# Fourier steps among conv2 in four groups instead of six, with changes of the prologue and of the work in front of conv2

## Chip, cores and metric

One core of a Trainium2 chip (trn2) runs the whole program. The metric is the device time of one execution in microseconds (us). TensorE (PE) does matrix products, VectorE (DVE) and ScalarE (ACT) elementwise work and copies out of PSUM, GpSimd (POOL) a part of the products of the prologue, SyncE (SP) issues most DMAs.

## Reference

x has 8 images of 32 channels of 64 x 64, float32. A first stage makes nine weights per pixel and blends each pixel's 3 x 3 neighbours with them; then come four layers (DEPTH = 4).

```python
# L0: h = leaky_relu(conv3x3(x, w1) + b1, 0.2)
#     w_lp = softmax(conv1x1(h, w2) + b2, axis=1)         # 9 weights a pixel
#     x = x + sum_k shift_k(x) * (delta_centre - w_lp[k])
for j in range(4):                                        # L1
    Kj, Lj = project(K[j]), project(L[j])                 # less their 3x3 mean
    z = relu(batchnorm(conv3x3(x, Kj), gamma[j], beta[j]))
    x = batchnorm(x + 0.1 * conv3x3T(z, Kj), gamma[j], beta[j])
    # diag_imp_conv_fft:
    t = 1.0 / (0.1 * abs(fft2(pad(Lj))) ** 2 + 1.0)
    x = real(ifft2(fft2(x) * t))
```

## The kernel before

The 8 images are taken as 4 pairs (bp), each pair in 4 quarters (q), so a stage has 16 chunks c = 4 bp + q (NCH = 16). The partitions hold 4 row groups (R) of 32 channels. X0 and Z0 hold x and z, X2 and Z2 copies that are shifted by two row groups (a DMA makes them), so that a 3 x 3 convolution of a chunk is 12 products of 128 rows by 32 columns, four of them side by side in the array (`conv`, L887; 24 MATMUL records a chunk).

Every product goes to one of 8 PSUM banks. The steps are numbered (`NUMBER`) in the order in which PE issues them; step n uses bank n % 8 and waits (`claim`) until step n - 8 is drained. The order is written by hand: `prologue_order` for the first stage and `layer_steps(j)` for a layer. Every engine walks the same list and does its own part of each step, so the list sets the order on PE, DVE and ACT alike.

**Prologue.** `hidden` p is the 3x3 convolution of two chunks (L910), `logits` the 1x1 one (L926), `less_max`, `exps` and `probabilities` make the softmax, which `cut` splits in three bf16 parts; `probsT` turns them (L939), `spread` copies each weight over the 32 channels by a product of 32 rows (L949), DVE and POOL multiply (L723, L421), and `sum` adds the 12 products of a chunk (L961). conv1 of layer 0 runs five chunks behind (BEHIND). SP and ACT issue the loads of x; b1 is loaded behind the first eight loads of SP (L353), and PE waits for `hconv_consts` 32 (w1 and b1) before its first product. ACT's order at the start is `keep_hidden(0)`, `keep_hidden(1)`, `exps(0)`, three `cut`s, `keep_probs(0)` and `(1)` (L486 to L493).

**A layer.** conv1 (16 chunks; DVE takes the statistics), with `prepare_taps` on DVE behind its seventh chunk. Then four `table` products (L987) of the filter's transform, each 12 rows by 128 columns by 512, with the product that spreads the means (`norm` 1, L995) in their middle. `scale_and_bias` on DVE (with a root on ACT) gives scale and bias of the batch norm; ReLU of z is then done in place, on ACT by `relu_pair` (L543), and for the shifted rows of the first chunk on DVE by `relu_first` (L800, L801). ACT squares the tables (L523), and DVE's `make_table` adds them and takes the reciprocal of 1,024 columns (L806 to L808), ahead of its first `add_conv2`. conv2 follows (L887 again; DVE adds the result to x, L815, and takes statistics, L818). Among its chunks stand the Fourier steps of the pairs that are done: `turn` (transpose, L1012, kept by ACT at L555), `fwdW` (transform along W, L1023), `fwdH` (along H, L1039, with `slot0`, L1032, in front and `slot0c`, L1047, behind it; DVE multiplies by the table), `invH` (L1057), `invW` (L1068). fwdW and invH come out of a bank in four copies a quarter (`keep_moved`: L568 on ACT, L824 on DVE); `by_dve` says who does it: DVE for fwdW of pairs 0 and 1 and the even quarters of the others, and for the odd quarters of invH of pairs 1 to 3. There is one buffer each for turned data (`turned`), the spectrum along W (`freqw`) and the whole spectrum (`spec`), and two for the way back (`backw`). Behind conv2 comes the second norm, whose scale `invW` (on ACT, L583) needs.

```python
    after = {
        5: fourier(j, 0, "turn"),
        7: fourier(j, 0, "fwdW"),
        9: fourier(j, 0, "fwdH") + fourier(j, 1, "turn"),
        11: fourier(j, 0, "invH") + fourier(j, 1, "fwdW"),
        13: fourier(j, 1, "fwdH") + fourier(j, 2, "turn"),
        15: fourier(j, 1, "invH") + fourier(j, 2, "fwdW"),
    }
```

## Time and profile before

| | us |
|---|---|
| median of 3 runs (lowest, highest) | 787.32 (786.62, 787.52) |
| the profiled execution, its own time | 783.87 |
| its span in the profile | 782.0 |
| PE busy | 741.6 (95%) |
| DVE busy | 479.6 (61%) |
| ACT busy | 387.5 (50%) |
| POOL busy | 95.6 (12%) |
| mean granted TensorE clock | 0.972 of full |
| prologue, up to the last conv1 of layer 0 | about 0 to 179.4 |
| a layer from its tables to the next layer's | about 158.7 |

The busy share says how long an engine had an instruction in flight, not that it ran at its peak. The granted clock is given as a share of 2.4 GHz: 1.00 is 2.4 GHz and 0.50 is 1.2 GHz, and a stretch between is a mixture of the two. Idle time is put down to what ended it.

### The profile page before, as it was taken

How to read it: one execution, taken by the hardware profiler on the slowest of the kernel's cores; microseconds unless marked ns; L12 is line 12 of the kernel's file. 1: busy time of each engine (PE TensorE's matmuls, PEld its weight loads, DVE VectorE, ACT ScalarE, POOL GpSimd, SP SyncE). 2: the span in 40 equal slices, each digit the busy share in tenths (PEclk: the TensorE clock that was granted, in tenths of full speed). 3: DMA queues.
4: the chain of work that ended last, by engine and by line, in shares of the span. 5: the costliest groups of instructions: out<-in, count | busy, mean ns of one | idle time of the engine just before them, and what ended most of it. 6: DMA issues, size and time to landing. Idle time of an engine off the chain costs nothing.

```text
span 782.0 us, 14876 instructions
## 1 busy us (share of the span) xinstructions
PE 741.6 (95%) x6016; PEld 374.5 (48%) x6016; DVE 479.6 (61%) x911; ACT 387.5 (50%) x703; POOL 95.6 (12%) x92
## 2 busy tenths in 40 slices
PE   4779999999999999999999999999999999999995
PEld 1223333222454875224558753235677542355785
DVE  2587887764957852448668533397676333877661
ACT  1465666636622655257135543491446433823564
POOL 0376666830000000000000000000000000000000
PEclk9798999999999999989999999999999998999998
DMA  9991111248000132840000427500004274000034
GB/s 182 188 164 29 29 30 28 56 92 191 2 1 1 31 80 61 187 118 2 1 1 1 110 56 166 145 1 1 1 2 111 55 166 110 1 1 1 2 88 129
DMA packets 44645, 51.16 MB, mean 65 GB/s; under 512 B 36385, under 2 KB 36514, under 8 KB 42530
## 3 DMA queue, kind: packets, MB, share of 16 engines
q1 hardware_dynamic: 40098, 48.92, 29.1%
q10 hardware_dynamic: 4480, 1.30, 1.1%
q8 instruction: 49, 0.80, 0.4%
q14 instruction: 18, 0.15, 0.1%
HBM read 11.92 MB, written 4.19 MB: 21 GB/s over the span
## 4 chain that ended last, share of the span: by engine, by line
PE 81%; DVE 10%; ACT 3%; issue 2%; DMA 1%; SPq 1%; POOL 0%; DVEq 0%; ACTq 0%; POOLq 0%
PE psum L887 39%; PE psum L1068 7%; PE psum L1039 7%; PE psum L961 6%; PE psum L1057 6%; PE psum L1023 6%; PE psum L910 3%; PE psum L1012 2%; PE psum L949 2%; DVE work L824 2%; DVE tabT L808 2%; DVE spare L824 2%; ACT Z L543 1%; PE psum L926 1%; DVE X L815 1%
## 5 line engine op out<-in xcount | busy, mean ns | idle before, releaser
L887 PE MATMUL psum<-Z,wts 128*32 128x512 f32 x1536 | 177.4, 615 | 5.1 <-DVE Z L801 5.1
L887 PE MATMUL psum<-X,wts 128*32 128x512 f32 x1536 | 170.1, 593 | 0.2 <-DMA X<-X 0.2
L824 DVE COPY work<-psum 64x256 f32<-64x256 f32 x224 | 94.5, 422 | 22.9 <-PE psum L1023 15.9
L734 DVE BATCH_NORM_STATS2 stats<-Z 128x6 f32<-128x512 f32 x60 | 41.5, 692 | 106.8 <-ACT Z L483 106.7
L887 PEld LDWEIGHTS psum<-Z,wts 128*32 128x32 f32 x1536 | 49.5, 112 | 118.3 <-issue 107.6
L887 PEld LDWEIGHTS psum<-X,wts 128*32 128x32 f32 x1536 | 47.4, 109 | 105.5 <-issue 103.1
L483 ACT ACTIVATE Z<-psum 128x512 f32<-128x512 f32 x64 | 38.3, 598 | 118.1 <-PE psum L887 107.0
L543 ACT ACTIVATE Z<-Z,small 64x128 f32<-64x128 f32 (+3 forms) x92 | 85.0, 973 | 5.2 <-DVE small L792 4.7
L568 ACT ACTIVATE work<-psum 64x256 f32<-64x256 f32 x160 | 61.4, 384 | 34.7 <-PE psum L1057 22.5
L815 DVE SCALAR_TENSOR_TENSOR X<-psum,X 128x512 f32<-128x512 f32 x64 | 43.7, 683 | 47.4 <-PE psum L887 47.0
L1057 PEld LDWEIGHTS psum<-cstS,work 128*128 128x128 f32 x512 | 58.4, 192 | 9.8 <-issue 9.8
L1057 PE MATMUL psum<-cstS,work 128*128 128x128 f32 x512 | 61.0, 277 | 0.5 <-ACT work L561 0.5
L1023 PE MATMUL psum<-cstS,work 128*128 128x128 f32 x512 | 60.2, 276 | 0.0
L1023 PEld LDWEIGHTS psum<-cstS,work 128*128 128x128 f32 x512 | 58.4, 192 | 3.4 <-issue 3.4
L561 ACT ACTIVATE work<-psum 128x64 f32<-128x64 f32 x16 | 4.6, 286 | 106.6 <-PE psum L1047 106.6
L1039 PE MATMUL psum<-work,cstS 128*128 128x496 f32 x128 | 56.3, 583 | 0.0
L842 DVE TENSOR_TENSOR work<-psum,tabT 128x496 f32<-128x496 f32 x64 | 41.2, 669 | 8.4 <-PE psum L1039 8.1
L818 DVE BATCH_NORM_STATS2 stats<-X 128x6 f32<-128x512 f32 x64 | 44.4, 694 | 2.2
L723 DVE TENSOR_TENSOR spare<-Z,psum 128x512 f32<-128x512 f32 x60 | 38.5, 679 | 11.9 <-PE psum L949 9.8
L723 DVE TENSOR_TENSOR work<-Z,psum 128x512 f32<-128x512 f32 x52 | 33.6, 680 | 16.0 <-PE psum L949 15.4
L583 ACT ACTIVATE X<-psum,small 128x512 f32<-128x512 f32 x48 | 36.1, 777 | 8.9 <-DVE small L792 3.6
L568 ACT ACTIVATE spare<-psum 64x256 f32<-64x256 f32 x64 | 24.9, 388 | 27.4 <-PE psum L1057 26.8
(104 smaller groups left out, 874.1 us busy)
## 6 DMA issues: line engine op xcount, KB each, us to landing
X<-X SPq DMA_DIRECT2D x64, 260.0 KB, 3.8
Z<-Z SPq DMA_DIRECT2D x32, 520.0 KB, 7.1
Z<-x SPq DMA_DIRECT2D x36, 128.0 KB, 5.0
out<-Z SPq DMA_DIRECT2D x24, 128.0 KB, 2.3
parS<-par SPq DMA_DIRECT2D x4, 673.0 KB, 8.2
Z<-x SPq DMA_DIRECT2D x12, 120.0 KB, 5.1
Z<-x ACTq DMA_DIRECT2D x14, 64.0 KB, 4.2
Z<-x SPq DMA_DIRECT2D x14, 64.0 KB, 4.8
```

The lines of the kernel that those rows point to most:

```text
L543: last = nc.scalar.activation(z, z, ACT.Relu, bias=small[p0:p1, 13:14], scale=small[p0:p1, 12:13])
L568: last = nc.scalar.activation(dst, src, ACT.Identity)
L723: nc.vector.tensor_tensor(by_line(product(c, dj, r)), around(c, dj, r), by_line(bank(n)), op=ALU.mult)\
L815: nc.vector.scalar_tensor_tensor(xc, in0=by_row(bank(n)), scalar=STEP, in1=xc, op0=ALU.mult, op1=ALU.add).then_inc(drained[n % BANKS], 1)
L818: return nc.vector.bn_stats(stats[:, 6 * c:6 * c + 6], xc)
L824: last = nc.vector.tensor_copy(dst, src)
L887: last = nc.tensor.matmul(out_b[C * r:C * r + C, :], weights[:, o:o + C], rows(src, reg, bp, g, CH, dj - 1), start=(dj == 0), stop=(dj == ...
L961: last = nc.tensor.matmul(bank(n)[C * r:C * r + C, :], cm(C_STACK, C), product(c, dj, r), start=(dj == 0), stop=(dj == 2), tile_position=( ...
L1023: last = nc.tensor.matmul(bank(n)[:, 128 * i:128 * i + 128], turned[:, p:p + 128], cm(C_FW), start=True, stop=True)
L1039: nc.tensor.matmul(bank(n)[:, 0:16 * (SL - 1)], cm(C_FH), freqw[:, N * q:N * q + N].rearrange("p (a s) -> p a s", s=SL)[:, :, 1:SL], start ...
L1057: last = nc.tensor.matmul(bank(n)[:, 128 * cp:128 * cp + 128], spec[:, p:p + 128], cm(C_IH), start=True, stop=True)
L1068: last = nc.tensor.matmul(bank(n)[:, 128 * g:128 * g + 128], backw[bp % 2][:, p:p + 128], cm(C_IW), start=True, stop=True)
```

## The change

1. Prologue. A product with w1 alone is issued 16 times (WARM) before PE waits for anything but w1; w1 gets a semaphore of its own. ACT runs one Prelu on a single column as soon as b1 is there. ACT does `keep_hidden(1)` behind the cuts of half 0 instead of ahead of `exps(0)`. The third `hidden` step moves from the end of chunk 0 to the middle of chunk 1 (HIDDEN_BEHIND), on PE and on ACT.
2. The taps and the table products use all 128 partitions; those beyond 12 hold zeros.
3. ReLU of the first pair is in three pieces, of 4, 4 and 8 row groups: ACT takes Z0, DVE all whole rows of Z2. conv2's chunks 0, 1 and 2 wait for a piece each.
4. `make_table` is split. `add_squares` stands behind chunk 0 of conv2, and the reciprocal is in four pieces of 256 columns behind chunks 1, 3, 5 and 6. `slot0` waits for all four. ACT waits for `squares_read` where it waited for `table_done`.
5. Fourier steps stand behind chunks 5, 9, 13 and 15 of conv2.

```diff
+INVERT_BEHIND = (1, 3, 5, 6)
+WARM = 16
+HIDDEN_BEHIND = (1, *range(2, 2 * PAIRS - 4, 2))
@@ def prologue_chunk(c):
+    if c == HIDDEN_BEHIND[0]:
+        order.append(("hidden", 2))
     order += spreads(c, 2)
-    if c % 2 == 0 and c // 2 + 2 < PAIRS:
-        order.append(("hidden", c // 2 + 2))
+    if c in HIDDEN_BEHIND[1:]:
+        order.append(("hidden", HIDDEN_BEHIND.index(c) + 2))
@@ def layer_steps(j):
         5: fourier(j, 0, "turn"),
-        7: fourier(j, 0, "fwdW"),
-        9: fourier(j, 0, "fwdH") + fourier(j, 1, "turn"),
-        11: fourier(j, 0, "invH") + fourier(j, 1, "fwdW"),
-        13: fourier(j, 1, "fwdH") + fourier(j, 2, "turn"),
-        15: fourier(j, 1, "invH") + fourier(j, 2, "fwdW"),
+        9: fourier(j, 0, "fwdW") + fourier(j, 1, "turn"),
+        13: fourier(j, 0, "fwdH") + fourier(j, 1, "fwdW") + fourier(j, 2, "turn"),
+        15: fourier(j, 0, "invH") + fourier(j, 1, "fwdH") + fourier(j, 2, "fwdW") + fourier(j, 1, "invH"),
@@ sync
-            sp.dma_start(w1S[:, :], w1).then_inc(hconv_consts, 16)
+            sp.dma_start(w1S[:, :], w1).then_inc(w1_in, 16)
@@ scalar
-            act.wait_ge(hconv_consts, 32)
+            act.wait_ge(hconv_consts, 16)
+            nc.scalar.activation(small[:, 24:25], b1S[:, 0:1], ACT.Prelu, alpha=LEAK)
             keep_hidden(0)
-            keep_hidden(1)
             exps(0)
             for i in range(3):
                 cut(0, i)
+            keep_hidden(1)
@@ def norm_relu(bp, g, n):
                 if g == 0:
                     parts.append((Z2, REG2, 0, 1, 2 * C, 128))
...
+                if bp:
+                    parts.append((Z2, REG2, g + 1, min(n, G - 1 - g), 0, 128))
+                if g + n == G:
+                    parts.append((Z2, REG2, G, 1, 0, 2 * C))
@@ def relu_pair(j, bp):
                 norm_relu(bp, 0, CH)
-                norm_relu(bp, CH, G - CH)
+                if bp == 0:
+                    norm_relu(bp, CH, CH)
+                    norm_relu(bp, 2 * CH, G - 2 * CH)
+                else:
+                    norm_relu(bp, CH, G - CH)
@@ vector: def relu_first(j)
-                z = rows(Z2, REG2, 0, 1, CH)
-                link(nc.vector.tensor_scalar(z, z, S(12), S(13), ALU.mult, ALU.add))
-                nc.vector.tensor_scalar(z, z, 0.0, None, ALU.max).then_inc(relu_by_dve, 1)
+                for g, n in ((1, CH), (1 + CH, CH), (1 + 2 * CH, G - 1 - 2 * CH)):
+                    z = rows(Z2, REG2, 0, g, n)
+                    link(nc.vector.tensor_scalar(z, z, S(12), S(13), ALU.mult, ALU.add))
+                    nc.vector.tensor_scalar(z, z, 0.0, None, ALU.max).then_inc(relu_by_dve, 1)
...
+            def invert(i):
+                t = tabT[:, 256 * i:256 * i + 256]
+                nc.vector.reciprocal(t, t).then_inc(table_done, 1)
@@ vector: steps of a layer
-                        make_table(j)
                     elif what == "conv2":
                         ins = add_conv2(*at)
+                        if at[1] == 0:
+                            add_squares(j)
+                        elif at[1] in INVERT_BEHIND:
+                            invert(INVERT_BEHIND.index(at[1]))
@@ tensor
+            pe.wait_ge(w1_in, 16)
+            for i in range(WARM):
+                nc.tensor.matmul(bank(NUMBER["logits", 1])[0:3 * C, 0:3 * C], w1S[:, :], w1S[:, :], start=True, stop=True)
             pe.wait_ge(zeroed, 1)
-            pe.wait_ge(hconv_consts, 32)
+            pe.wait_ge(hconv_consts, 16)
@@ def table(j, i):
-                nc.tensor.matmul(bank(n), cm(e, k=12), taps[:, N * (i % 2):N * (i % 2) + N], start=True,
+                nc.tensor.matmul(bank(n), cm(e), taps[:, N * (i % 2):N * (i % 2) + N], start=True,
@@ def conv2(j, c):
-                if c == 0:
-                    pe.wait_ge(relu_by_dve, j + 1)
-                if c % Q < 2:
-                    pe.wait_ge(relu_done, 2 * BP * j + 2 * (c // Q) + 1 + c % Q)
+                bp, q = divmod(c, Q)
+                if bp == 0 and q < 3:
+                    pe.wait_ge(relu_by_dve, 3 * j + q + 1)
+                    pe.wait_ge(relu_done, (2 * BP + 1) * j + q + 1)
+                elif q < 2:
+                    pe.wait_ge(relu_done, (2 * BP + 1) * j + 2 * bp + q + 2)
```

How it moves instructions: PE among conv2 of a layer, from the tables to the second norm. `X,wts` is conv1 and `Z,wts` conv2 (x12 is one chunk), `cstS,X` turn, `cstS,work` of L1023 fwdW and of L1057 invH, 128x496 fwdH, 128x64 slot0 or slot0c, `small` a norm. Before:

```order
L887 MATMUL psum<-Z,wts 32x512 x72
L1012 MATMUL psum<-cstS,X 128x128 x16
L887 MATMUL psum<-Z,wts 32x512 x24
L1023 MATMUL psum<-cstS,work 128x128 x16
L887 MATMUL psum<-Z,wts 32x512 x24
L1032 MATMUL psum<-work,cstS 128x64
L1039 MATMUL psum<-work,cstS 128x496 x4
L1047 MATMUL psum<-work,cstS 128x64
L1012 MATMUL psum<-cstS,X 128x128 x16
L887 MATMUL psum<-Z,wts 32x512 x24
L1057 MATMUL psum<-cstS,work 128x128 x16
L1023 MATMUL psum<-cstS,work 128x128 x16
```

And after, where fwdW is L1057, turn L1046, fwdH L1073 and invH L1091, from the second group to the second norm's step:

```order
L915 MATMUL psum<-Z,wts 32x512 x48
L1057 MATMUL psum<-cstS,work 128x128 x16
L1046 MATMUL psum<-cstS,X 128x128 x16
L915 MATMUL psum<-Z,wts 32x512 x48
L1066 MATMUL psum<-work,cstS 128x64
L1073 MATMUL psum<-work,cstS 128x496 x4
L1081 MATMUL psum<-work,cstS 128x64
L1057 MATMUL psum<-cstS,work 128x128 x16
L1046 MATMUL psum<-cstS,X 128x128 x16
L915 MATMUL psum<-Z,wts 32x512 x24
L1091 MATMUL psum<-cstS,work 128x128 x16
```

Between two groups PE now does four conv2 chunks (x48) where it did two (x24), and the last group behind chunk 15 starts with invH of pair 0. ACT's start of the program, before:

```order
L437 ACT_TABLE_LOAD
L437 ACTIVATE work<-psum,b1S 128x512 x2
L443 ACTIVATE work<-work 128x288
L450 ACTIVATE work<-work 128x32x9 x3
L457 ACTIVATE work<-psum 128x512 x2
```

And after (with the tiles' numbers kept apart: work0 takes `keep_hidden`, work1 `exps`, work3 the cuts and `keep_probs`):

```order
L498 ACT_TABLE_LOAD
L498 ACTIVATE small<-b1S 128x1
L447 ACTIVATE work0<-psum,b1S 128x512
L453 ACTIVATE work1<-work1 128x288
L460 ACTIVATE work3<-work2 128x32x9 x3
L447 ACTIVATE work0<-psum,b1S 128x512
L467 ACTIVATE work3<-psum 128x512 x2
```

The table load has gone ahead of the first `keep_hidden`, and the second `keep_hidden` behind the three cuts.

## Rows read from the trace of the kernel before

**Rows 1.** The page: PE's busy time, and the chain that ended last, by engine.
```profile
PE 741.6 (95%) x6016; PEld 374.5 (48%) x6016; DVE 479.6 (61%) x911; ACT 387.5 (50%) x703; POOL 95.6 (12%) x92
...
PE 81%; DVE 10%; ACT 3%; issue 2%; DMA 1%; SPq 1%; POOL 0%; DVEq 0%; ACTq 0%; POOLq 0%
```

**Rows 2.** Busy time by stretch: start:end, length, PE, PEld, DVE, ACT, POOL; then PEclk.
```profile
184.90:188.30 3.40, 3.17 (x16) 0.90 (x20) 0.00 (x0) 3.37 (x4) 0.00 (x0) 0.50 1.00 213
...
338.50:341.90 3.40, 3.40 (x10) 1.33 (x8) 2.42 (x12) 0.89 (x2) 0.00 (x0) 1.00 0.37 78
341.90:348.70 6.80, 5.56 (x25) 1.35 (x28) 1.37 (x4) 6.29 (x9) 0.00 (x0) 0.50 0.82 219
```

**Rows 3.** Timeline of PE, fronts of conv2, layers 0 to 3: start us, length us.
```profile
185.13 17.21 PE L887 MATMUL psum<-Z,wts 128*32 128x512 f32 x144 [1.50 <-DVE Z L801]
...
203.98 0.63 PE L1012 MATMUL psum<-cstS,X 128*128 128x128 f32 x4 [0.18 <-DVE X L815]
...
343.78 18.09 PE L887 MATMUL psum<-Z,wts 128*32 128x512 f32 x144 [1.24 <-DVE Z L801]
...
502.95 17.02 PE L887 MATMUL psum<-Z,wts 128*32 128x512 f32 x144 [1.51 <-DVE Z L801]
...
661.60 17.90 PE L887 MATMUL psum<-Z,wts 128*32 128x512 f32 x144 [0.86 <-DVE Z L801]
```

**Rows 4.** The chain that ended last, layer 0: start us, length us, what.
```profile
209.90 3.77 PE psum L1023 x32
...
218.96 0.40 PE psum L1032 x2
...
222.87 1.75 PE psum L1012 x16
...
233.68 3.57 PE psum L1023 x32
...
248.22 5.33 PE psum L887 x48
...
263.49 3.34 PE psum L1039 x8
...
312.25 25.90 PE psum L887 x240
```

**Rows 5.** Groups by line: busy us, mean ns | idle before, releaser.
```profile
L824 DVE COPY work<-psum 64x256 f32<-64x256 f32 x224 | 94.5, 422 | 22.9 <-PE psum L1023 15.9 <-PE psum L1057 3.3
...
L568 ACT ACTIVATE work<-psum 64x256 f32<-64x256 f32 x160 | 61.4, 384 | 34.7 <-PE psum L1057 22.5 <-PE psum L1023 10.3
...
L815 DVE SCALAR_TENSOR_TENSOR X<-psum,X 128x512 f32<-128x512 f32 x64 | 43.7, 683 | 47.4 <-PE psum L887 47.0
...
L555 ACT ACTIVATE work<-psum 128x512 f32<-128x512 f32 x64 | 33.3, 602 | 9.7 <-PE psum L1012 9.6
...
L808 DVE RECIPROCAL tabT<-tabT 128x1024 f32<-128x1024 f32 x4 | 26.2, 6553 | 0.1
...
L800 DVE TENSOR_SCALAR Z<-Z,small 128x512 f32<-128x512 f32 x4 | 2.2, 548 | 0.1
```

**Rows 6.** Timeline of ACT, front of conv2 in layer 0.
```profile
183.71 4.85 ACT L543 ACTIVATE Z<-Z,small 128x512 f32<-128x512 f32 x5 [1.18 <-DVE small L792]
```

**Rows 7.** The chain that ended last, start of the program.
```profile
9.92 4.93 PE psum L910 x24
14.93 1.28 ACT L437
...
16.96 1.40 PE psum L926 x8
...
23.18 0.34 ACT work L443
...
28.87 0.61 PE psum L949
```

**Rows 8.** The page: loads of x in half groups, KB each, us to landing.
```profile
Z<-x SPq DMA_DIRECT2D x14, 64.0 KB, 4.8
```

More of the change, by code:

```diff
@@ L168, in build @@
         turned, freqw, spec, rest, backw0 = work
-        taps = rest[0:12, 0:C * SL]
+        taps = rest[:, 0:C * SL]
         slot0 = rest[:, C * SL:C * SL + 2 * C]
@@ L185, in build @@
         ksum = sb("ksum", 2 * C)
-        lsum = sb("lsum", 6 * C, parts=12)
+        lsum = sb("lsum", 6 * C)
         extra = sb("extra", N)
@@ L213, in build @@
         drained = [sem(f"bank_drained{i}") for i in range(BANKS)]
+        w1_in = sem("w1_in")
         hconv_consts = sem("hconv_consts")
@@ L241, in build @@
         relu_done = sem("relu_done")
+        squares_read = sem("squares_read")
         table_done = sem("table_done")
@@ L506, in _ @@
                     keep_conv1(0, c - BEHIND)
+                if c == HIDDEN_BEHIND[0]:
+                    keep_hidden(2)
                 copy_weights(c, 2)
@@ L509, in _ @@
                     cut(c // 2 + 1, 0)
-                if c % 2 == 0 and c // 2 + 2 < PAIRS:
-                    keep_hidden(c // 2 + 2)
+                if c in HIDDEN_BEHIND[1:]:
+                    keep_hidden(HIDDEN_BEHIND.index(c) + 2)
                 if c % 2 and c + 1 < NCH:
@@ L648, in prepare_taps @@
                 al, be = lsum[:, 4 * C:5 * C], lsum[:, 5 * C:6 * C]
-                link(nc.vector.tensor_reduce(ml, parS[0:12, P_L9:P_ALL].rearrange("p (c t) -> p c t", t=TAPS),
+                link(nc.vector.tensor_reduce(ml, parS[:, P_L9:P_ALL].rearrange("p (c t) -> p c t", t=TAPS),
                                              op=ALU.add, axis=AX))
-                link(nc.vector.scalar_tensor_tensor(row, in0=ml.unsqueeze(2).broadcast_to([12, C, 3]), scalar=-1.0 / TAPS,
-                                                    in1=parS[0:12, P_L:P_L9].rearrange("p (c t) -> p c t", t=3),
+                link(nc.vector.scalar_tensor_tensor(row, in0=ml.unsqueeze(2).broadcast_to([128, C, 3]), scalar=-1.0 / TAPS,
+                                                    in1=parS[:, P_L:P_L9].rearrange("p (c t) -> p c t", t=3),
                                                     op0=ALU.mult, op1=ALU.add))
-                nc.vector.tensor_scalar(al, row[:, :, 1], cstS[0:12, C_ONE:C_ONE + 1], None, ALU.mult)
-                link(nc.vector.scalar_tensor_tensor(be, in0=row[:, :, 0], scalar=cstS[0:12, C_SGN:C_SGN + 1],
+                nc.vector.tensor_scalar(al, row[:, :, 1], cstS[:, C_ONE:C_ONE + 1], None, ALU.mult)
+                link(nc.vector.scalar_tensor_tensor(be, in0=row[:, :, 0], scalar=cstS[:, C_SGN:C_SGN + 1],
                                                     in1=row[:, :, 2], op0=ALU.mult, op1=ALU.add))
                 t3 = taps[:, :].rearrange("p (c s) -> p c s", s=SL)
-                link(nc.vector.tensor_tensor(t3, be.unsqueeze(2).broadcast_to([12, C, SL]),
-                                             cstS[0:12, C_CS:C_CS + SL].unsqueeze(1).broadcast_to([12, C, SL]),
+                link(nc.vector.tensor_tensor(t3, be.unsqueeze(2).broadcast_to([128, C, SL]),
+                                             cstS[:, C_CS:C_CS + SL].unsqueeze(1).broadcast_to([128, C, SL]),
                                              op=ALU.mult))
-                nc.vector.tensor_tensor(t3, t3, al.unsqueeze(2).broadcast_to([12, C, SL]), op=ALU.add)\
+                nc.vector.tensor_tensor(t3, t3, al.unsqueeze(2).broadcast_to([128, C, SL]), op=ALU.add)\
                     .then_inc(prep_done, 1)
@@ L798, in relu_first, with add_squares @@
                 dve.wait_ge(z2_in[0], 32 * (j + 1))
-                z = rows(Z2, REG2, 0, 1, CH)
-                link(nc.vector.tensor_scalar(z, z, S(12), S(13), ALU.mult, ALU.add))
-                nc.vector.tensor_scalar(z, z, 0.0, None, ALU.max).then_inc(relu_by_dve, 1)
-            def make_table(j):
+                for g, n in ((1, CH), (1 + CH, CH), (1 + 2 * CH, G - 1 - 2 * CH)):
+                    z = rows(Z2, REG2, 0, g, n)
+                    link(nc.vector.tensor_scalar(z, z, S(12), S(13), ALU.mult, ALU.add))
+                    nc.vector.tensor_scalar(z, z, 0.0, None, ALU.max).then_inc(relu_by_dve, 1)
+            def add_squares(j):
                 for i in range(4):
                     bk.result(NUMBER["table", j, i])
-                link(nc.vector.tensor_tensor(tabT[:, :], turned[:, 0:1024], turned[:, 1024:2048], op=ALU.add))
+                nc.vector.tensor_tensor(tabT[:, :], turned[:, 0:1024], turned[:, 1024:2048], op=ALU.add)\
+                    .then_inc(squares_read, 1)
+                dve.wait_ge(squares_read, j + 1)
                 link(nc.vector.tensor_scalar(tabT[:, :], tabT[:, :], STEP, 1.0, ALU.mult, ALU.add))
-                nc.vector.reciprocal(tabT[:, :], tabT[:, :]).then_inc(table_done, 1)
-                dve.wait_ge(table_done, j + 1)
+            def invert(i):
+                t = tabT[:, 256 * i:256 * i + 256]
+                nc.vector.reciprocal(t, t).then_inc(table_done, 1)
             def add_conv2(j, c):
@@ L861, in _ @@
                     elif what == "slot0":
+                        if at[1] == 0:
+                            dve.wait_ge(table_done, 4 * (j + 1))
                         scale_slot0(*at)
```

8 lines of the change are left out of this document (1 added, 7 removed).

## The prediction

> **What bounds the kernel now.** I read the page first: PE has an instruction in flight 95% of the span, and 81% of the chain that ended last is PE's [rows 1]. So a microsecond counts only if PE is shortened, sped up or spared a wait. Then I looked for three things on PE: stretches in which its clock is halved, waits, and what a change between conv products and 128 x 128 products costs.
>
> The stretches by granted clock show the first. In layer 1 PE is busy 3.40 of 3.40 us from 338.5 to 341.9, nearly all of it table products of 12 rows, and the clock is halved from 341.9 to 348.7, where conv2 begins; in layer 0 it is halved from 184.9 to 188.3, with PE busy for 3.17 us of it [rows 2]. The timeline of PE gives the price. The first six conv2 chunks of a layer take 17.21, 18.09, 17.02 and 17.90 us [rows 3], while ten conv1 chunks, which are the same products, take 25.90 us at full clock, 2.59 each [rows 4]; six at that pace are 15.6. Behind them the fourth quarter of turn waits for DVE's addition, 0.18 us in layer 0 [rows 3] and the like in layer 2: DVE has just spent 6.55 us in one reciprocal [rows 5].
>
> The second is the chain in a layer. fwdW behind conv2 takes 3.77 us, and behind other full products 3.57 [rows 4]. Two conv2 chunks behind full products take 5.33 us, against 5.18 for two from the row of ten [rows 4]. So one trip out of conv2 and back costs 0.20 + 0.15, some 0.35 us (a little less in most, say 0.32). At the second norm, chunk 15 ends at 248.22 + 5.33 = 253.55 and fwdH starts at 263.49, 9.94 us later [rows 4]. PE's work between is invH 3.77, fwdW 3.57, turn 1.75, slot0 0.2 (its 0.40 less the 0.20 of leaving conv2) and the norm's small product, some 0.1: 9.4. Half a microsecond is a wait, for DVE's last fwdW copies.
>
> The third is the start. The first hidden product takes 4.93 us though it has the products of a conv chunk, ACT then loads a table for 1.28, logits run at 16.96 for 1.40, the exponential waits until 23.18 because ACT keeps hidden 1 first, and the first spread product starts at 28.87 [rows 7].
>
> **The change, part by part.** The sum is made against the profiled execution, 783.87 us (span 782.0), which is 3.45 below the median of 787.32; I subtract the same gain from the median.
>
> *Front of conv2.* PE's table products are as many and as long with 128 rows as with 12 (both stream 512 columns), and DVE's instructions on the taps are as many, in the shadow of conv1's 25.90 us [rows 4]; without that shadow they would still be only four short instructions and two of 1,024 elements a layer. What changes is the clock. I read the halving as the answer to few rows at work plus the idle 0.86 to 1.51 us ahead of conv2 [rows 3]: in layer 1 PE was never idle in the 3.4 us before the fall, so idleness alone doesn't explain it [rows 2]. With 128 rows that stretch is as full as conv1, and I take it that the clock stays at 2.4 GHz. The idle time in front of chunk 0 stays, since chunk 0 still waits for the norm and the first ReLU pieces. Chunk 1 used to wait for all of ACT's 4.85 us of ReLU [rows 6], hidden now only by the slow clock; the new pieces end earlier. ACT has less than 4.85 us for the pair. DVE has two more pieces, of 4 and 7 row groups, two passes each at 0.55 us or less per 4 groups [rows 5]: under 3 us more, done about 4 us behind its start, when chunk 0 (2.6 us) is just ending. The reciprocal in pieces is 6.55 / 4 = 1.64 us each; An addition with its statistics is twice 0.68 us, some 1.4 [rows 5]. Turn needs four of them, and with the ReLU (some 4), the table's sum (some 2) and the reciprocal piece behind chunk 1 DVE has 5.5 + 4 + 2 + 1.6 = 13 us of work in the 15.6 of the six chunks. The other pieces and the fifth and sixth additions lie beside turn and chunk 6 and are done before fwdH, which now comes behind chunk 13. So the gain is 17.21 + 18.09 + 17.02 + 17.90 = 70.2, less 0.3 by which the timeline overlaps the next row, less 4 x 15.6 = 62.4: 7.5; with the waits at turn, some 0.5 in all, and some 0.3 of turn behind conv2, **8.3 us**. Ends: 0.5 if the clock still halves; 9.5 if idle time shrinks too.
>
> The Trainium skill, "TensorE: Matmul & The Clock Gate" (What's actually happening), says that the gate follows how busy PE has recently been and says nothing of rows. By that rule zeros in more rows would change nothing, and the sum would have 0.5 for this part. The trace speaks against it as far as it goes: PE was busy throughout 338.5 to 341.9 [rows 2].
>
> *Four groups.* Two trips a layer go: 2 x 0.32 x 4 = 2.6 us. The wait at the second norm goes too, as invH of pair 1 and turn of pair 3 (3.57 + 1.75) now stand between fwdW and fwdH of pair 2: 0.5 x 4 = 2.0. What may take their place is bank traffic. Behind chunk 15 PE has invH 3.77, fwdH with its slots 3.7, fwdW 3.57, invH 3.57 and turn 1.75, in all 16.4 us. ACT has invH of pair 0 (16 copies), half of fwdW and of invH of pair 1 (8 each), that is 32 copies at 0.384 = 12.3, four kept turns at 0.602 = 2.4 and slot0c (a small copy, some 0.3): 15.0 us [rows 5]. DVE has 16 copies at 0.422 = 6.8, four scalings and chunk 15 at 0.7 a pass with its aggregate, some 12. Followed quarter by quarter, ACT ends invH of pair 0 at 7.3 us and PE wants that bank for the second quarter of fwdW at 8.4; the tightest later ones have some 1 us as well. DVE's seven microseconds of fwdW copies in the groups behind 9 and 13 lie beside conv2 chunks that find their banks free. **4.6 us**; ends 0 and 5.5.
>
> *Prologue.* The warming products run from about 3 us (w1's landing) to about 8 and delay nothing, as PE waits for b1 until 9.92. If PE is then at 2.4 GHz, hidden 0 takes 2.7 instead of 4.93: 2.2 us; if not, 0. The table load of 1.28 goes under the wait for b1. The exponential follows logits 0 by the 1.0 us of two DVE steps, where it came 23.18 - 18.36 = 4.8 behind [rows 7]: 3.8. Against that hidden 1 is kept (0.7, as from 16.2 to 16.96) and logits 1 runs (1.4) in front of the first transposes: minus 2.1. Hidden 1 can't start before the second half of its loads, which land 4.8 us behind an issue at about 11 [rows 8], near 15.5 to 16; that is before the cuts are done, so it costs nothing. The third hidden step (2.7 us at full clock) moves from a place where DVE's products hid it to one where they do so in part; I take 0, between -1.5 and +2. No DMA is moved in any queue. From about 70 us on PE is the bound, and what is gained stays. Sum 2.2 + 1.3 + 3.8 - 2.1 = 5.2; I take **5 us**, from 1.5 to 8, since the clock is also halved twice for 6.8 us before 70 us and may or may not be so in a shifted prologue.
>
> Sum: 8.3 + 4.6 + 5 = 17.9. 783.9 - 17.9 = 766.0 for a profile like this one; 787.3 - 17.9 = **769.4** for the median.
>
> **Rivals.**
> 1. *The clock still halves in front of conv2*, because what counts is busy time (the rule of the Trainium skill above), or the idle 1.2 to 1.5 us. For it: idle time stays. Against it: layer 1 before 341.9. Gain 0.5 + 4.6 + 5 = 10.1, **777.2**. Chance 0.2.
> 2. *The start gives little*: PE is slow again when b1 lands, and another halved stretch falls in, so the prologue gives 1.5. **772.9**. Chance 0.15.
> 3. *The groups are bound by banks*: PE waits a microsecond or so behind chunk 15, and the 4.6 are given back. **774.0**. Chance 0.08.
> 4. *Slower than before*: ACT falls behind in the group behind chunk 15. It has 15.0 us of work beside 16.4 of PE's. To eat all of 17.9 us PE must wait 4.5 us a layer more, and for that ACT's 32 copies would have to take 0.57 us instead of 0.384 with DVE and ACT copying at once: (15.0 + 5.9) - 16.4 = 4.5. At 0.60 us the time would be **791**. Against it: ACT and DVE copy side by side before too, and the mean is 0.384. Chance 0.03.
> 5. *The change doesn't do what it says*: clock, norm and start all stay as they are, and only the trips go, 2.6 us: **784.7**. Chance 0.04.
>
> **How the numbers follow.** The forecast has the remaining 0.5. Its own range, from the terms' ends without the rivals, is 765 to 773. Rivals 1 to 3 lie up to 777; so the range is 764 to 778, with rivals 4 and 5 and some of the tails left out. A measurement of this kernel can tell about 0.2% (1.6 us) from no change. Only rival 4 is slower; a mixture of rivals 5 and others could end within 0.2%: faster 0.95, same 0.02, slower 0.03.
>
> **What would show it.** Granted clock 1.00 from the tables to chunk 6 in all layers, and six chunks in 15.7 us instead of 17 to 18; if they still take 17, rival 1. Conv2 rows of x96 between groups and no idle time at fwdH behind the second norm; idle time of PE there released by ACT's copies would be rivals 3 and 4. The first hidden row at 2.7 to 2.8 us, the first spread near 23.5 and the last conv1 of layer 0 ending near 174.5 instead of 179.5. I am wrong if PE shows new waits longer than 0.5 us a layer, or if the time is over 778.

## The result, and the profile after

| | before | changed |
|---|---|---|
| median, us (lowest to highest, 4 runs each) | 786.97 (785.08 to 787.52) | 767.63 (766.45 to 767.79) |
| ratio, with 95% interval | | 0.9755 (0.9736 to 0.9775) |
| profiled execution, us | 783.87 | 767.67 |
| its span, us | 782.0 | 765.5 |

The change takes 19.3 us off the median; 17.9 were forecast (769.4, range 764 to 778). The two profiled executions differ by 16.2 only, because the one of before was quicker than any of its timed runs. In four later batches of runs the kernel before had medians of 784.72 to 786.66, against which the gain would be 17.1 to 19.0, so the last microsecond or two of the 19.3 is not certain. The page of the changed kernel, PE's busy time, the granted clock in 40 slices and the chain:

```profile
PE 732.8 (96%) x6048; PEld 381.4 (50%) x6048; DVE 493.1 (64%) x939; ACT 382.9 (50%) x704; POOL 95.6 (12%) x92
...
PEclk9698999999999999999999999999999999999999
...
PE 91%; DVE 3%; issue 2%; ACT 1%; DMA 1%; SPq 1%; POOL 0%; ACTq 0%; DVEq 0%; POOLq 0%
```

PE has 9 us less in flight and 32 records more (the warming products), and its share of the chain went from 81% [rows 1] to 91%: DVE's part fell from 10% to 3%. From 62.4 to 762 us the clock is never below full.

The timeline of PE in the fronts of conv2, layers 0 and 1, to be read against [rows 3]:

```profile
176.19 1.98 PE L1019 MATMUL psum<-work,cstS 128*128 128x512 f32 x4
178.06 0.36 PE L1027 MATMUL psum<-small,cstS 128*128 128x5 f32 x2
178.28 1.96 PE L1019 MATMUL psum<-work,cstS 128*128 128x512 f32 x4
181.83 15.67 PE L915 MATMUL psum<-Z,wts 128*32 128x512 f32 x144 [1.58 <-DVE Z L820]
...
331.82 1.98 PE L1019 MATMUL psum<-work,cstS 128*128 128x512 f32 x4
...
337.46 15.67 PE L915 MATMUL psum<-Z,wts 128*32 128x512 f32 x144 [1.59 <-DVE Z L820]
353.06 1.97 PE L1046 MATMUL psum<-cstS,X 128*128 128x128 f32 x16
```

Six chunks take 15.67 us in every layer, where they took 17.02 to 18.09, and turn follows without a wait. The idle time ahead of chunk 0 is still there, 1.58 us. From the tables of one layer to those of the next it is now 155.63 us each time (331.82 - 176.19); before it was 158.7 to 159.2. With the last layer, which has no next one (122.4 us from its tables to the end, before 126.1), that is 13.3 us of the spans' 16.5; the other 3.2 lie ahead of the first tables. Busy time and clock in the same stretch of layer 0, to be read against [rows 2] (columns as there):

```profile
176.20:179.60 3.40, 3.40 (x13) 1.57 (x10) 2.42 (x10) 0.89 (x2) 0.00 (x0) 1.00 1.00 208
179.60:183.00 3.40, 1.81 (x14) 0.50 (x16) 3.19 (x9) 2.55 (x4) 0.00 (x0) 1.00 1.05 225
```

PE is less busy from 179.6 to 183.0 than it was in layer 1 of before ahead of its fall, and the clock stays at 1.00 of 2.4 GHz. The chain in the groups of layer 0, to be read against [rows 4]:

```profile
199.40 10.44 PE psum L915 x96
209.84 3.77 PE psum L1057 x32
213.61 1.75 PE psum L1046 x16
215.35 10.44 PE psum L915 x96
...
240.37 3.77 PE psum L1091 x32
...
255.06 1.75 PE psum L1046 x16
256.81 0.12 PE psum L1027 x2
256.93 0.31 PE psum L1066 x2
257.24 3.34 PE psum L1073 x8
```

Four chunks stand together (x96, 10.44 us), and at the second norm fwdH follows the norm's product without a wait. From the start of chunk 6 to this fwdH it is 57.84 us. Before it was 263.49 - 204.61 = 58.88, where 204.61 is the start of chunk 6 in the chain. ACT in the steps behind chunk 15, whose last product ends at 240.37:

```profile
241.50 6.41 ACT L585 ACTIVATE work<-psum 64x256 f32<-64x256 f32 x16 [5.62 <-PE psum L1091]
...
249.74 1.55 ACT L585 ACTIVATE work<-psum 64x256 f32<-64x256 f32 x4 [1.51 <-PE psum L1057]
...
256.32 2.06 ACT L572 ACTIVATE work<-psum 128x512 f32<-128x512 f32 x4
```

It ends invH of pair 0 at 247.91, 7.5 us in (7.3 were worked out), is idle for 1.5 us behind a small copy, and keeps the last turn at 258.38 while PE is in fwdH.

The start, PE's timeline, to be read against [rows 7]:

```profile
9.73 2.78 PE L938 MATMUL psum<-Z,w1S 128*32 128x512 f32 x24 [1.76 <-DMA b1S<-b]
...
13.31 1.11 PE L954 MATMUL psum<-w2S,work 128*128 128x72 f32 x8
15.37 2.78 PE L938 MATMUL psum<-Z,w1S 128*32 128x512 f32 x24 [0.95 <-DMA Z<-x]
...
20.66 1.62 PE L954 MATMUL psum<-w2S,work 128*128 128x72 f32 x8 [1.83 <-ACT work L447]
...
23.40 1.03 PE L977 MATMUL psum<-work,selS 32*128 32x512 bf16 x5 [0.26 <-ACT work L467]
```

Hidden 0 takes 2.78 us instead of 4.9, and the first spread starts at 23.40 instead of 28.87. The last conv1 of layer 0 ends only 3.2 us earlier, though (the tables start at 176.19 against 179.42). The clock was halved for longer than before:

```profile
21.40:35.00 13.60, 9.15 (x53) 3.25 (x52) 9.54 (x17) 6.16 (x12) 5.99 (x5) 0.51 1.28 191
```

That is 13.6 us in one piece, twice as long as the longest such stretch in the prologue before. The fourth hidden step, in the changed kernel and in the one before:

```profile
45.34 2.78 PE L938 MATMUL psum<-Z,w1S 128*32 128x512 f32 x24
```

```profile
48.51 2.78 PE L910 MATMUL psum<-Z,w1S 128*32 128x512 f32 x24
```

By this step the lead of 5.5 us at the first spread is down to 3.2, and it stays so: from there to the tables both kernels take 130.9 us.

### The profile page after: what moved, and what is told of

Read it like the earlier page. It is cut to its first block, busy times and chain, and to the rows that moved or that the text cites. A ratio compares the mean times of both kernels' runs of the same rounds, so it can differ in the third digit from the quotient of the medians.

```text
span 765.5 us, 14976 instructions
## 1 busy us (share of the span) xinstructions
PE 732.8 (96%) x6048; PEld 381.4 (50%) x6048; DVE 493.1 (64%) x939; ACT 382.9 (50%) x704; POOL 95.6 (12%) x92
## 4 chain that ended last, share of the span: by engine, by line
PE 91%; DVE 3%; issue 2%; ACT 1%; DMA 1%; SPq 1%; POOL 0%; ACTq 0%; DVEq 0%; POOLq 0%
PE psum L915 43%; PE psum L1091 8%; PE psum L1102 8%; PE psum L1057 8%; PE psum L1073 7%; PE psum L989 6%; PE psum L1046 4%; PE psum L938 2%; PE psum L977 2%; PE psum L954 1%; PE psum L1019 1%; PE psum L1066 1%; DMA b1S<-b 1%; PE psum L949 1%; DMA X<-X 1%
## 5 line engine op out<-in xcount | busy, mean ns | idle before, releaser
L915 PE MATMUL psum<-Z,wts 128*32 128x512 f32 x1536 | 168.2, 593 | 6.3 <-DVE Z L820 6.3
L915 PEld LDWEIGHTS psum<-Z,wts 128*32 128x32 f32 x1536 | 51.7, 109 | 113.7 <-issue 102.0
L556 ACT ACTIVATE Z<-Z,small 128x512 f32<-128x512 f32 (+4 forms) x92 | 80.4, 924 | 5.2 <-DVE small L810 4.7
L1091 PEld LDWEIGHTS psum<-cstS,work 128*128 128x128 f32 x512 | 58.4, 192 | 6.4 <-issue 6.4
L1091 PE MATMUL psum<-cstS,work 128*128 128x128 f32 x512 | 60.6, 277 | 0.5 <-ACT work L578 0.5
L1057 PE MATMUL psum<-cstS,work 128*128 128x128 f32 x512 | 60.6, 277 | 0.0
L1057 PEld LDWEIGHTS psum<-cstS,work 128*128 128x128 f32 x512 | 58.4, 192 | 3.4 <-issue 3.4
L572 ACT ACTIVATE work<-psum 128x512 f32<-128x512 f32 x64 | 33.0, 602 | 54.0 <-PE psum L1046 53.9
L1073 PE MATMUL psum<-work,cstS 128*128 128x496 f32 x128 | 56.3, 582 | 0.0
L865 DVE TENSOR_TENSOR work<-psum,tabT 128x496 f32<-128x496 f32 x64 | 42.8, 674 | 13.7 <-PE psum L1073 13.7
```

Source lines behind the costliest of these rows:

```text
L556: last = nc.scalar.activation(z, z, ACT.Relu, bias=small[p0:p1, 13:14], scale=small[p0:p1, 12:13])
L915: last = nc.tensor.matmul(out_b[C * r:C * r + C, :], weights[:, o:o + C], rows(src, reg, bp, g, CH, dj - 1), start=(dj == 0), stop=(dj == ...
L1057: last = nc.tensor.matmul(bank(n)[:, 128 * i:128 * i + 128], turned[:, p:p + 128], cm(C_FW), start=True, stop=True)
L1073: nc.tensor.matmul(bank(n)[:, 0:16 * (SL - 1)], cm(C_FH), freqw[:, N * q:N * q + N].rearrange("p (a s) -> p a s", s=SL)[:, :, 1:SL], start ...
L1091: last = nc.tensor.matmul(bank(n)[:, 128 * cp:128 * cp + 128], spec[:, p:p + 128], cm(C_IH), start=True, stop=True)
```

## The experiments

Twelve more kernels ran. Five of them and the changed kernel share one prologue word for word, so their profiles also show how far the same start varies: the tables of layer 0 begin at 176.19 (changed), 174.44, 176.36, 177.59, 177.91 and 176.34 in those compared (the kernels with fills of the prologue are not among them). That is 3.5 us with the same code up to there. Comparisons of a layer's length, which in the changed kernel repeats to 0.1 us, are therefore sharper than medians, and I give both. The changed kernel was timed in one batch only, and the runs come from two chips, so a difference of a microsecond between two medians says little.

### Table products on 12 rows again

```diff
-                nc.tensor.matmul(bank(n), cm(e), taps[:, N * (i % 2):N * (i % 2) + N], start=True,
+                nc.tensor.matmul(bank(n), cm(e, k=12), taps[0:12, N * (i % 2):N * (i % 2) + N], start=True,
```

> The changed kernel with the table products back on 12 rows; the taps are still made on all partitions. Theory R (few rows at work let the clock fall): the clock is halved again in front of conv2 in every layer for 3.4 or 6.8 us, the first six chunks of conv2 take 17 to 18 us instead of 15.7, and the time is 7 to 8 us above the changed kernel's 767.6, near 775. Rival I (it is the idle 1.2 to 1.6 us in front of conv2 and PE's busy time that set the clock, and the split ReLU and table mended it): clock 1.00 there and 767.6 within 1 us.

Measured: 774.18 us, ratio to before 0.9857 (0.9838 to 0.9876), 6.6 us over the changed kernel. The timeline of PE in layer 1, and two stretches in layer 0:

```profile
335.82 1.98 PE L1019 MATMUL psum<-work,cstS 12*128 12x512 f32 x4
339.30 17.09 PE L915 MATMUL psum<-Z,wts 128*32 128x512 f32 x144 [1.50 <-DVE Z L820]
```

```profile
178.60:182.00 3.40, 1.96 (x5) 0.65 (x4) 2.90 (x13) 1.60 (x4) 0.00 (x0) 0.97 1.01 210
182.00:185.40 3.40, 3.33 (x20) 0.98 (x24) 1.96 (x4) 3.40 (x6) 0.00 (x0) 0.53 1.02 220
```

PE's instructions, their lengths and its idle time ahead of chunk 0 (1.50 against 1.58) are those of the changed kernel; only 116 rows of zeros are gone. The clock falls in every layer again, for 3.4 us each time, and six chunks take 17.0 to 17.2 us. The layer is 157.1 us long instead of 155.63, 6.0 us over four layers; the medians' 6.6 is a little under the 7 to 8 expected. Theory R holds, rival I falls.

### Table products on 128 rows alone

```diff
-        taps = rest[0:12, 0:C * SL]
+        taps = rest[:, 0:C * SL]
...
-                nc.tensor.matmul(bank(n), cm(e, k=12), taps[:, N * (i % 2):N * (i % 2) + N], start=True,
+                nc.tensor.matmul(bank(n), cm(e), taps[:, N * (i % 2):N * (i % 2) + N], start=True,
```

(`prepare_taps` is as in the change.)

> The kernel before with nothing changed but the taps and table products on 128 partitions. Theory R and D (R as above; D: DVE's reciprocal of 1,024 columns ahead of its additions ends at the same moment whatever PE's clock): clock 1.00 in front of conv2, six chunks in some 16 us, but turn then waits some 1.5 us for DVE's fourth addition, which ends when it ended before; gain 0 to 2 us, near 786. Rival P (the clock alone was the price): 7 to 8 us faster, near 779. Rival I: clock still halved, time as before.

Measured: 783.44 us, 0.9973 (0.9961 to 0.9986): 3 us faster than before. PE's timeline in layer 0:

```profile
185.96 2.78 PE L888 MATMUL psum<-Z,wts 128*32 128x512 f32 x24 [1.59 <-DVE Z L802]
189.44 13.09 PE L888 MATMUL psum<-Z,wts 128*32 128x512 f32 x120 [0.70 <-ACT Z L543]
202.46 1.66 PE L1013 MATMUL psum<-cstS,X 128*128 128x128 f32 x12
204.80 0.63 PE L1013 MATMUL psum<-cstS,X 128*128 128x128 f32 x4 [0.69 <-DVE X L816]
```

The clock is full (chunk 0 in 2.78 us), and two waits stand where the slow clock was: 0.70 us of chunk 1 for ACT's ReLU and 0.69 of turn's last quarter for DVE's addition. The clock speaks for R and against I, and the gain, far from 7 to 8, against P. D is right only in part: turn waits 0.69 us where 1.5 were expected, and the wait of chunk 1 wasn't in it. The gain of 3 is above its 0 to 2. In the traces, though, the layer is 158.6 us long against 158.7 and 159.2 before, 1.4 us over four layers; from the start of chunk 0 to that of chunk 6 it takes 19.40 us, where two of the four layers before took 19.41. The two waits ate nearly all that the clock gave.

### Table whole, ahead of DVE's additions

```diff
                         relu_first(j)
+                        add_squares(j)
+                        for i in range(4):
+                            invert(i)
...
-                        if at[1] == 0:
-                            add_squares(j)
-                        elif at[1] in INVERT_BEHIND:
-                            invert(INVERT_BEHIND.index(at[1]))
```

> The changed kernel with the sum of squares and all four reciprocal pieces on DVE ahead of its first conv2 addition, as before the change. Theory D (turn waits for DVE): clock 1.00, six chunks in 15.7 us, but turn's last quarter waits for the fourth addition as before, 1.5 to 2 us a layer, 6 to 8 in all, near 775. Rival C (with the clock at full the table is hidden anyway): under 1 us.

Measured: 767.96 us, 0.9778 (0.9757 to 0.9798), 0.3 us over the changed kernel by the medians. In the trace the layer is 156.22 us long, 0.6 more, 2.4 over four layers: the medians would be rival C, the layers lie between it and theory D. PE's timeline in layer 1:

```profile
353.82 1.53 PE L1045 MATMUL psum<-cstS,X 128*128 128x128 f32 x12
355.75 0.63 PE L1045 MATMUL psum<-cstS,X 128*128 128x128 f32 x4 [0.40 <-DVE X L838]
```

Turn does wait, but for 0.40 us, not 1.5 to 2. What I had missed: the new ReLU is shorter on ACT (3.68 us of L556 for the first pair against 4.85 [rows 6]), so the squares are ready earlier: in layer 0 DVE's sum of squares starts 5.8 us behind the end of `scale_and_bias` (180.53 to 186.30), where before it was 6.9 (183.68 to 190.61). That takes 1.1 us off the 1.5 that I had expected. So some of what I had put on the split reciprocal belongs to the split ReLU.

### ReLU in two parts as before

```diff
-                for g, n in ((1, CH), (1 + CH, CH), (1 + 2 * CH, G - 1 - 2 * CH)):
-                    z = rows(Z2, REG2, 0, g, n)
+                z = rows(Z2, REG2, 0, 1, CH)
...
-                if bp:
+                if bp or g:
                     parts.append((Z2, REG2, g + 1, min(n, G - 1 - g), 0, 128))
```

(and ACT's pieces and PE's waits as before)

> The changed kernel with ReLU of the first pair in two parts as before (DVE 4 row groups of Z2, ACT the rest), all else as changed. Theory: chunk 1 of conv2 waits some 0.7 us for ACT's longer ReLU, as it did in the kernel before with 128 rows; the split reciprocal keeps turn from waiting; 2.8 us over four layers, near 770.4. Rival (only the order of the table counts): within 0.5 us of 767.6. Rival (squares 1.2 us later push DVE's additions past turn): 5 us or more.

Measured: 772.32 us, 0.9833 (0.9818 to 0.9848), 4.7 over the changed kernel by the medians; the layer is 156.53 us long, 0.9 more, 3.6 over four layers. PE's timeline in layer 1:

```profile
340.09 2.78 PE L910 MATMUL psum<-Z,wts 128*32 128x512 f32 x24 [1.59 <-DVE Z L815]
343.57 13.09 PE L910 MATMUL psum<-Z,wts 128*32 128x512 f32 x120 [0.70 <-ACT Z L556]
356.59 1.97 PE L1040 MATMUL psum<-cstS,X 128*128 128x128 f32 x16
```

Chunk 1 waits 0.70 us, as theory said, and turn doesn't wait. The rest of the layer's 0.9 is that the six chunks now start twice: 2.78 and 13.09 are 0.2 us more than 15.67. With the table undone too (the kernel of 128 rows alone) chunk 0 to chunk 6 takes 19.40 us, 1.90 more than the changed kernel's 17.50, where the two undone singly cost 0.91 and 0.60.

### A fill behind table products of 12 rows

```diff
+            def fill(n, times):
+                bk.claim(n)
+                for i in range(times):
+                    nc.tensor.matmul(bank(n)[:, 0:128], cm(C_ID), cm(C_ID), start=True, stop=True)
...
                 bp, q = divmod(c, Q)
+                if c == 0:
+                    fill(NUMBER["conv2", j, c], 6)
```

(on top of the 12-row kernel)

> The changed kernel with table products on 12 rows, and six products of 128 rows by 128 columns (a fill, results overwritten) in PE's idle time between the tables and chunk 0 of conv2, 1.3 of the 1.6 us. If what PE does with all its rows sets the clock: it stays at 1.00 in front of conv2 in most layers and the time is back near 768 against 774.2 without the fill. If products on 12 rows lower the clock by themselves, whatever stands behind them: 774.

Measured: 775.75 us, 0.9873 (0.9844 to 0.9901), runs from 772.49 to 779.17; the layer is 157.2 us long, as without the fill. PE's timeline in layer 0 and a stretch inside it:

```profile
179.82 1.98 PE L1024 MATMUL psum<-work,cstS 12*128 12x512 f32 x4
181.73 2.81 PE L932 MATMUL psum<-cstS 128*128 128x128 f32 x12
184.47 16.06 PE L915 MATMUL psum<-Z,wts 128*32 128x512 f32 x144
```

```profile
182.00:183.00 1.00, 1.00 (x6) 1.00 (x6) 0.97 (x3) 0.99 (x2) 0.00 (x0) 0.50 1.11 225
```

PE is not idle at all between the last conv1 and conv2, and the clock falls all the same, right behind the 12-row products. The fill then runs at 1.2 GHz, takes 2.81 us where turn's twelve records of the same shape take 1.53 at full clock, and holds chunk 0 back. So in this kernel idle time is not needed for the fall; products on 12 rows alone in that stretch are enough. Which mixture of the two would keep the clock is not settled by it.

### Six groups again, and four groups alone

```diff
-        9: fourier(j, 0, "fwdW") + fourier(j, 1, "turn"),
-        13: fourier(j, 0, "fwdH") + fourier(j, 1, "fwdW") + fourier(j, 2, "turn"),
-        15: fourier(j, 0, "invH") + fourier(j, 1, "fwdH") + fourier(j, 2, "fwdW") + fourier(j, 1, "invH"),
+        7: fourier(j, 0, "fwdW"),
+        9: fourier(j, 0, "fwdH") + fourier(j, 1, "turn"),
+        11: fourier(j, 0, "invH") + fourier(j, 1, "fwdW"),
+        13: fourier(j, 1, "fwdH") + fourier(j, 2, "turn"),
+        15: fourier(j, 1, "invH") + fourier(j, 2, "fwdW"),
```

> The changed kernel with the Fourier steps back in six groups (behind chunks 5, 7, 9, 11, 13, 15). Theory: two trips out of conv2 and back a layer at 0.3 us, and the wait of about 0.5 us for DVE's fwdW copies at the second norm; 1.05 us a layer, 4.2 in all, near 771.8. Rival (the order only moves waits, what is left is the trips): 2.5 us, near 770.1. Rival (four groups lose as much at the banks as they save): 0.

Measured: 771.96 us, 0.9823 (0.9804 to 0.9843), 4.3 over the changed kernel. The layer is 156.68 us long, 1.05 more, the amount that was worked out. PE's timeline has the wait at the second norm back:

```profile
255.46 0.28 PE L1029 MATMUL psum<-small,cstS 128*128 128x5 f32 x2
256.09 0.44 PE L1068 MATMUL psum<-work,cstS 128*128 128x64 f32 x2 [0.34 <-DVE work L849]
256.35 3.52 PE L1075 MATMUL psum<-work,cstS 128*128 128x496 f32 x8
```

The same edit, the other way round, on the kernel before:

> The kernel before with the four groups alone. Theory: the groups' gain is a thing of its own, 4.2 us, near 782.8. Rival: behind a late front of conv2 DVE is behind with its additions and the group behind chunk 9 waits for it, gain under 2 us.

Measured: 782.33 us, 0.9945 (0.9923 to 0.9967), 4.2 faster than before, though six chunks still take 17.02 to 18.31 us. In its trace the stretch from chunk 6 to fwdH of the second norm is as short as in the changed kernel in all four layers, 57.73 us by the starts in the timeline, where it was 58.77. The groups' gain is a thing of its own, and no rival of either run is left.

### The prologue, one part at a time

No warming products:

```diff
-WARM = 16
+WARM = 0
```

> The changed kernel without the 16 warming products. Theory: the first hidden product runs at 1.2 GHz again, 4.9 us instead of 2.8, all that follows it starts 2.1 us later, and about 2 us reach the end: near 769.7. Rival (the second half of the loads, hidden 1 from 15.4 us on, hides it): 0 to 1 us.

Measured: 770.28 us, 0.9804 (0.9784 to 0.9824), 2.7 over the changed kernel. PE's timeline:

```profile
10.12 5.35 PE L938 MATMUL psum<-Z,w1S 128*32 128x512 f32 x24 [10.12 <-DMA b1S<-b]
```

Hidden 0 takes 5.35 us, and the first spread starts at 26.70 instead of 23.40, the tables at 178.58 instead of 176.19; the price is somewhat over the 2 us expected. ACT keeps hidden 1 first again:

```diff
             keep_hidden(0)
+            keep_hidden(1)
             exps(0)
             for i in range(3):
                 cut(0, i)
-            keep_hidden(1)
```

> The changed kernel with ACT keeping hidden 1 ahead of the first exponential again. Theory: the exponential waits for hidden 1, which waits for its loads until 15.4 us: it comes at 18.8 instead of 15.4, 3.4 us later; logits 1 is then no longer in front of the first transposes, 1.6 us back; 1.7 us slower, near 769.3. Rival: DVE or a longer halved clock takes it in, 0.

Measured: 769.97 us, 0.9795 (0.9773 to 0.9816), 2.3 over. Its PE timeline:

```profile
9.83 4.43 PE L938 MATMUL psum<-Z,w1S 128*32 128x512 f32 x24 [2.40 <-DMA b1S<-b]
```

The first spread starts at 25.46. Here hidden 0 took 4.43 us in spite of the warming, which is 1.65 of these 2.1 us. Two other profiles have ACT's new order and a slow hidden 0 (4.23 and 4.31 us), and their first spread starts at 24.63 and 25.65. So what the order alone is worth isn't shown: the medians say 2.3, and no trace separates it from the slow step. Warming doesn't always hold: of the ten profiles with it, hidden 0 took 2.78 us in seven, where PE had been idle for 1.20 to 1.86 us ahead of it, and 4.2 to 4.4 in three, where it had been idle for 2.04 to 2.62. The third hidden step back at the end of chunk 0:

```diff
-    if c == HIDDEN_BEHIND[0]:
-        order.append(("hidden", 2))
     order += spreads(c, 2)
+    if c == 0:
+        order.append(("hidden", 2))
```

(and `keep_hidden(2)` likewise)

> The changed kernel with the third hidden step back at the end of chunk 0. Theory: it must wait for loads that land near 29.5 us while the first sum stands behind it; the first sum ends some 2 to 3 us later, and 1 us of it is left at the end, near 768.6. Rival (the place of this step doesn't matter): within 0.5 us of 767.6.

Measured: 771.63 us, 0.9814 (0.9793 to 0.9834), 4.0 over the changed kernel, four times what I expected. PE's timeline:

```profile
30.82 5.35 PE L938 MATMUL psum<-Z,w1S 128*32 128x512 f32 x24 [4.25 <-DMA Z<-x]
```

PE stands for 4.25 us, waiting for the loads, and then does the step at half clock, 5.35 us instead of 2.78; the tables start at 180.25, 4.1 us later. With the start moved forward the loads of the second pair have become what is late next; moving the step is what lets the rest of the gain through.

### Fills in the prologue

```diff
+                if h == 1:
+                    fill(n, 10)
@@ turn_probs
+                if c == 4:
+                    fill(n, 8)
@@ add_up
+                if c == 0:
+                    fill(n, 12)
```

(`fill` repeats the warming product into the step's own bank. In an execution of the changed kernel a second stretch of halved clock, 6.8 us long, follows near 56 us.)

> The changed kernel with fills in PE's idle times of the prologue: 10 products of 96 columns ahead of logits 1, 12 ahead of the first sum, 8 ahead of the transposes of chunk 4; all results are overwritten. Theory (the 13.7 us of halved clock from 21.4 on, and the 6.8 from 55.5 on, come of idle PE): part of the halved time goes, the last conv1 of layer 0 ends 2 to 3 us earlier, near 765. Rival (the start is bound by DVE, ACT and the loads, not PE's clock): 767 to 768, or slower by the fills' own time, up to 2 us.

Measured: 768.30 us, 0.9786 (0.9769 to 0.9803), no faster than the changed kernel. Its timeline of PE:

```profile
19.87 1.94 PE L932 MATMUL psum<-w1S 128*96 128x96 f32 x20
...
31.76 4.13 PE L932 MATMUL psum<-w1S 128*96 128x96 f32 x24 [2.24 <-DVE spare L741]
```

The mean clock rose from 0.984 to 0.989, but the fill ahead of the first sum ran at 1.2 GHz for 4.13 us and held the sum back until 35.8, where it had started at 30.9. With half the first fill and without that one:

> The changed kernel with fewer fills than in the run before: 5 products of 96 columns ahead of logits 1 and 8 ahead of the transposes of chunk 4, none ahead of the first sum, whose fill ran at half clock and held that sum back. Theory: the second halved stretch (6.8 us near 56) goes and nothing is held back; 1 to 2 us faster than the changed kernel, near 766. Rival (by then DVE's products set the pace of the start, so PE's clock buys nothing): 767 to 768.

Measured: 767.61 us, 0.9765 (0.9744 to 0.9786). This can't be told from the changed kernel (0.9755). The mean clock is 0.988 and the second halved stretch is gone:

```profile
24.60:38.20 13.60, 9.85 (x59) 2.46 (x63) 10.07 (x18) 6.44 (x13) 8.18 (x7) 0.60 1.26 194
38.40:75.00 36.60, 34.22 (x302) 13.12 (x301) 31.70 (x54) 22.69 (x43) 27.14 (x25) 1.00 0.69 108
```

The rival was that DVE's products set the pace there and PE's clock buys nothing; DVE is busy for 31.70 of the 36.6 us in which the clock is full. But the trace goes against it: the tables start at 174.34, 1.9 us earlier than in the changed kernel, and from the fourth hidden step to the tables it takes 128.8 to 128.9 us in both runs with fills, where the second stretch is gone, against 130.9 in the changed kernel, where it is there. So that stretch costs some 2 us, as theory had it, and its profiled execution took 766.00. Why the median of the five runs shows nothing of it (766.00 to 768.02) stays open, as only one of them was traced. No version here beats the changed kernel by the medians.

## Why the prediction was right, point by point

**The front of conv2: 8.3 us forecast, 8.5 measured.** This is measured in the profiled pair. From the start of chunk 0 to that of chunk 6 the four layers took 19.41, 19.92, 19.41 and 19.74 us, the differences of those starts in the timeline before; now it is 17.50 (199.33 - 181.83) each. 78.5 - 70.0 = 8.5. The reading of the clock was right and is now shown as far as the rows go: with 12 rows it falls, with 128 it doesn't, and nothing else differs. The second half of the reading, that the idle time ahead of conv2 has a part in it, isn't: with 12 rows the clock falls without that idle time too. The end of 9.5 for a shorter idle time wasn't reached; it stayed at 1.58.

The rival with chance 0.2, that busy time alone counts, had the rule of the Trainium skill, "TensorE: Matmul & The Clock Gate" (What's actually happening), beside it. The runs decide against that reading, if busy means an instruction in flight: PE was busy alike with 12 and with 128 rows, at 6.6 us between them. The same page of the Trainium skill (Why this matters for your kernels) names long idle gaps of PE between bursts of products as what drops the clock. With full rows a gap of 1.58 us left it at 1.00, which doesn't go against that; with 12 rows it falls without any gap, which isn't covered by it.

**The shares inside the front were only half right.** I had named the wait of chunk 1 for ACT's ReLU correctly (0.70 us with the clock at full, 2.8 of the layers' 3.6). For the reciprocal I had argued from DVE's end time alone and expected 6 to 8 us if it went back; it was 0.3 by medians and 2.4 by the trace, because I had left out that ACT's shorter ReLU moves the squares, and with them the table, forward. The shares are also not sums. From chunk 0 to chunk 6, over four layers, the traces of the kernel before, of the two runs on table rows and of the changed kernel have:

| | ReLU and table as before | both split |
|---|---|---|
| 12 rows | 78.5 us (before) | 75.7 us |
| 128 rows | 77.6 us | 70.0 us (changed) |

The clock alone gives 0.9 us, the two splits alone 2.8, and both together 8.5.

**The groups: 4.6 forecast, 4.2 measured** (1.04 us a layer in the trace, 4.3 and 4.2 by the two runs). Both terms were a little large. From chunk 6 to the product of the second norm layer 0 took 57.89 us before and takes 57.31 now, so a trip is 0.29 us and not 0.32. From that product to slot0 it took 0.62 us and takes 0.15 now, so the wait was worth 0.47 us and not 0.5. The bank traffic behind chunk 15 came out as worked out as far as ACT's end of invH goes, and PE never waits there for ACT. Rivals 3 and 4 fell with that.

**The prologue: 5 forecast, 3.2 measured** in the profiled pair (179.42 - 176.19). The start itself was as drawn: hidden 0 in 2.78 us, the first spread at 23.40 (23.5 forecast). What failed comes behind it: the sum carried the lead at the first spread through to 70 us whole, but 2.3 us are lost between the first spread and the fourth hidden step, which are 21.9 us apart (before 19.6), and the tables start at 176.2 where 174.5 stood. A part of it is the clock, which I had left open as luck. The kernel with six groups has the same prologue and started its tables at 174.44; between these two steps its mean granted clock was 0.84 (before 0.85, changed kernel 0.74), and they are 21.0 us apart. That leaves 0.9 us to the longer halved stretch and 1.4 to something else. The term that I suspect is the 0 for the third hidden step: before, PE did it while DVE's products ahead of the first sum weren't ready, and now it stands idle for 2.20 us there and does the step later. No run shows this by itself. The 0 also had the wrong reason: its old place would have cost 4 us in the new start, for it would have waited for loads and not been hidden by DVE.

**The sum was closer than its terms.** The profiled pair differs by 8.5 in the fronts, 4.2 in the groups and 3.2 in the prologue, by 0.3 ahead of chunk 0 and by 0.3 at the end of the last layer: 16.5 us, 1.4 less than forecast, with the prologue 1.8 short by itself. The median moved by 1.4 more than forecast. That it lies so near is in part luck: the four timed runs of before have the highest median of its five batches, and no trace shows where they spent the 3.1 us that they took beyond the traced execution. The prediction's own range had a slip too: the upper ends of its terms add up to 23.0 and give 764.3, not 765.

**The parts don't add up.** Undone one at a time they cost 6.6 (rows), 4.7 (ReLU), 0.3 (table), 4.3 (groups), 2.7 (warming), 2.3 (ACT's order) and 4.0 (the hidden step), in all 24.9 us by the medians, where 19.3 were gained. By the layers' lengths the first four cost 6.0, 3.6, 2.4 and 4.2, in all 16.2 where 13.3 were gained. Done alone, the rows bring 3.0 by the medians and 1.4 by the layers, where undoing them costs 6.6 and 6.0: alone, the clock's gain runs into the two waits that the slow clock had covered.

## What to carry to other kernels

A halved clock covers waits: when it goes, look up what ended just before the slow work did, here ACT's ReLU and DVE's table, and mend both together or most of the gain stays there. Before sums are made on a start that is moved forward, ask which loads it will meet. And where an order has slack, fewer changes between kinds of product are worth about 0.3 us each on PE, provided the copies of the longer group are counted quarter by quarter against the banks.
